# Adding expert rows to the output in DRAM with accumulating DMAs in place of a gather back

## What is computed

```python
logits = xf @ Wr + br                      # xf: the normalised 2048 rows
topv, topi = jax.lax.top_k(logits, 2)      # two of eight experts for each row
gates = jax.nn.softmax(topv, axis=-1)
...                                        # rank of each row in its expert; rows of rank >= 512 are dropped
h = jax.nn.gelu(jnp.einsum('ecd,edh->ech', xg, W1) + b1[:, None, :], approximate=False)
out = jnp.einsum('ech,ehd->ecd', h, W2) + b2[:, None, :]
weighted = out * w[..., None]
final = jnp.zeros((N + 1, C), xf.dtype).at[buf.reshape(-1)].add(weighted.reshape(-1, C))
...
x = x + final
```

## Time and profile before

| what | value |
|---|---|
| median of 3 runs | 2440.91 us (2438.87 to 2442.47) |
| span of the profiled execution | 2439.1 us |
| TensorE matmuls | 2070.7 us busy, 85% of the span |
| VectorE | 1749.3 us busy, 72% |
| ScalarE | 1053.5 us busy, 43% |
| GpSimd | 291.1 us busy, 12% |
| DMA traffic | 102.79 MB, mean 42 GB/s |
| mean granted TensorE clock | 0.912 of full speed |

### The profile page before, as it was taken

The page is one execution under the profiler, slowest core; times in us unless marked ns, Lnnn a source line. Parts: engine busy times, 40 slices in busy tenths (PEclk is TensorE's granted clock), DMA queues, the critical chain, the costliest instruction groups (busy, mean ns, idle before and its releaser), DMA issues. The chain is left out here.

```text
span 2439.1 us, 33598 instructions
## 1 busy us (share of the span) xinstructions
PE 2070.7 (85%) x12304; PEld 1268.9 (52%) x12304; DVE 1749.3 (72%) x2604; ACT 1053.5 (43%) x1646; POOL 291.1 (12%) x332
## 2 busy tenths in 40 slices
PE   4999999999999999884669778988798888669994
PEld 3666666666666666541224444444444445546662
DVE  6677777777777788769999989989899984210002
ACT  1222222222222222338666876576758842212220
POOL 1111111111111111100000000010010001310005
PEclk8999999999999999997869888978799996769997
DMA  6000000000000100011111110111101102103333
GB/s 235 2 1 18 27 26 1 18 27 26 1 18 27 31 1 1 1 56 41 52 41 36 42 52 24 37 41 35 35 24 54 52 18 78 44 20 108 108 116 112
DMA packets 57485, 102.79 MB, mean 42 GB/s; under 512 B 7828, under 2 KB 39087, under 8 KB 56832
## 3 DMA queue, kind: packets, MB, share of 16 engines
q1 hardware_dynamic: 54272, 93.67, 11.6%
q0 software_dynamic: 3072, 7.28, 1.0%
HBM read 87.10 MB, written 14.94 MB: 42 GB/s over the span
## 5 line engine op out<-in xcount | busy, mean ns | idle before, releaser
L1983 PE MATMUL pa<-arena 128*128 128x512 f32 x512 | 303.1, 722 | 93.4 <-DVE arena L1499 93.1
L1491 DVE TENSOR_TENSOR_SCAN arena<-arena 128x1024 f32<-128x1024 f32 x128 | 292.3, 2284 | 9.4 <-ACT arena L885 9.0
L1713 PE MATMUL po<-arena 128*128 128x256 f32 x960 | 224.2, 385 | 0.0
L1983 PEld LDWEIGHTS pa<-arena 128*128 128x128 f32 x512 | 102.7, 220 | 227.2 <-DVE arena L1499 125.8
L1703 PE MATMUL pa<-arena 128*128 128x512 f32 x480 | 212.4, 594 | 4.0 <-ACT arena L705 3.7
L553 POOL TENSOR_SCALAR arena<-arena 128x2 f32<-128x2 f32 (+1 forms) x92 | 27.7, 301 | 1513.9 <-DVE arena L1355 835.5
L1171 DVE TENSOR_TENSOR arena<-pa,arena 128x512 f32<-128x512 f32 x256 | 158.6, 681 | 67.3 <-PE pa L1661 67.2
L727 ACT COPY arena<-pa 128x512 f32<-128x512 f32 x128 | 65.7, 600 | 324.9 <-PE pa L1661 324.9
L869 ACT ACTIVATE arena<-arena 128x510 f32<-128x510 f32 x256 | 170.5, 717 | 59.4 <-DVE arena L1491 51.3
L1713 PEld LDWEIGHTS po<-arena 128*128 128x128 f32 x960 | 176.8, 189 | 32.8 <-issue 6.0
L1618 DVE TENSOR_TENSOR arena<-po,arena 128x512 f32<-128x512 f32 x16 | 11.1, 692 | 243.3 <-PE po L2252 217.5
(11 more groups left out here) (255 smaller groups left out, 3685.8 us busy)
## 6 DMA issues: line engine op xcount, KB each, us to landing
arena<-bc_rows SPq DMA_DIRECT2D x64, 512.0 KB, 4.4
arena<-in_L_ffn_W SPq DMA_DIRECT2D x16, 1024.0 KB, 7.3
arena<-in_L_attn_W SPq DMA_DIRECT2D x8, 1024.0 KB, 5.5
rows_to_experts<-arena SPq DMA_DIRECT2D x4, 1024.0 KB, 12.7
arena<-rows_to_experts SPq DMA_DIRECT2D x8, 512.0 KB, 8.8
rows_from_experts<-arena SPq DMA_DIRECT2D x8, 512.0 KB, 3.3
arena<-in_x SPq DMA_DIRECT2D x4, 512.0 KB, 7.6
arena<-in_rows SPq DMA_DIRECT2D x8, 256.0 KB, 3.1
```

The lines of the kernel that those rows point to most:

```text
L1491: v.tensor_tensor_scan(h.rearrange(flat), decay.rearrange(flat), h.rearrange(flat), 0.0, ALU.mult, ALU.add).then_inc(scan_done, 1)
L1713: last = mm(po[s][:, ts(i, D)], gT[:, c, ts(tile, P)], w2[:, c, :], start=c == 0, stop=c == FM - 1)
L1983: last = mm(pa[c][:, :], ident, uh[i % len(uh)][:, n, :], start=g == 0 and n == 0, stop=g == NS // NG - 1 and n == NG - 1)
```

## The change

The result is added up in DRAM. `out` gets 512 rows more behind its 2048, which serve as targets for empty slots and are cut off at the end.

- Each slot has a tag of two numbers: its token's row in `out` and its gate. A DRAM tensor `tags_to_experts` is first filled (row N + slot number within the expert, gate 0). After the last row scatter GpSimd writes tags with 32 indirect DMAs of 128 x 8 bytes, to the same slots as the rows.
- `weighed` only computes the two gates; zeroing, slot sorting and `share` are gone.
- SyncE stores x (`xst`) to `out` as soon as each pair's rows have their final value, behind the weight loads of experts 0 and 1, and one store fills the 512 extra rows. It waits for `tags_sent` behind the row loads of experts 0 and 1, then loads their slot tags; for later experts the tags follow the rows.
- VectorE gates each expert's rows in place: after an eviction (now signalled by `down3_out`, on which TensorE waits) it multiplies each of the four tiles by the gate of its slots, and signals `ye_ready` per tile. A small operation turns the tags' row numbers into integers. For expert 0 both evictions come ahead of the wait for tags.
- GpSimd adds each tile to `out` with an indirect DMA that accumulates (`compute_op=ALU.add`), four for each expert, and waits before each expert for the adds of the one before. At the end it waits for all of them.
- The gather back, the sums on VectorE, the store of expert rows and the last stores of `out` are gone.

```diff
--- before.py
+++ after.py
@@ -49,7 +49,7 @@
 HEAD_STEPS, TAIL_STEPS, CROSS_STEPS = 47, 5, 22
 CROSS_SLOTS = 38
-ROUTED_EARLY = 43
+ROUTED_EARLY = 36
 VALUE_COPIES = (0, 1, 6, 8)
@@ -325,21 +325,21 @@
     above, level = a(NT, NE, NE), a(NT, NE, NE)
     picked, before, rank = a(NT, NE), a(NT, NE), a(NT, NE)
-    lt, gate, rk, base, over, place = ([a(NT) for _ in range(2)] for _ in range(6))
-    order, part, share = ([a(NT) for _ in range(2)] for _ in range(3))
+    lt, rk, base, over = ([a(NT) for _ in range(2)] for _ in range(4))
+    tags = [a(NT, 2) for _ in range(2)]
+    gate = [one[:, :, 1] for one in tags]
     gexp = a(NT)
     into = [a(NT).bitcast(I32) for _ in range(2)]
-    outof = [a(NT).bitcast(I32) for _ in range(2)]
+    slot_tags, slot_rows = [a(TT, 2) for _ in range(2)], [a(TT).bitcast(I32) for _ in range(2)]
     weights_at = a.at
-    back = [a(NT, D) for _ in range(2)]
     assert a.at <= ARENA, a.at
     bc_rows = nc.dram_tensor("bc_rows", (BC, W), F32, kind="Internal").ap()
-    rows_back = nc.dram_tensor("rows_from_experts", (NE * CAP, D), F32, kind="Internal").ap()
+    tags_to = nc.dram_tensor("tags_to_experts", (NE * CAP, 2), F32, kind="Internal").ap()
     pa = [ctx.enter_context(nc.psum_tensor(f"pa{i}", [P, 512], F32)) for i in range(4)]
@@ -403,9 +403,9 @@
     logits_ready, sel_ready, rank_done, lt_ready, gexp_ready, places_ready = (
     scattered, tr3_done, tr3_out, up3_done, gelu3_ready = (sem(n) for n in ("scattered", "tr3_done", "tr3_out", "up3_done", "gelu3_ready"))
-    we_in, xg_in, down3_done, ye_ready, ye_kept = ([sem(f"{n}{j}") for j in range(2)] for n in ("we_in", "xg_in", "down3_done", "ye_ready", "ye_kept"))
-    back_in = [[sem(f"back_in{k}_{p}") for p in range(PAIRS)] for k in range(2)]
-    order_ready, final_ready = sem("order_ready"), sem("final_ready")
+    we_in, xg_in, down3_done, ye_ready, ye_added = ([sem(f"{n}{j}") for j in range(2)] for n in ("we_in", "xg_in", "down3_done", "ye_ready", "ye_added"))
+    down3_out, tags_in = ([sem(f"{n}{j}") for j in range(2)] for n in ("down3_out", "tags_in"))
+    tokens_in, tags_set, tags_ready, tags_sent, slot_rows_ready = sem("tokens_in"), sem("tags_set"), sem("tags_ready"), sem("tags_sent"), sem("slot_rows_ready")
     HELD[0] = sem("held")
     LAST = L * PAIRS
@@ -463,6 +463,7 @@
         for q in range(4):
+        sp.dma_start(tags_to, t["tags"]).then_inc(tags_set, 16)
         for dst, name in ((w_sv, "sim_wv"), (w_gate, "gate"), (w_pair, "pair_w"), (w_in, "ssm_in"), (w_xp, "ssm_xp"),
             sp.dma_start(dst, t[name].rearrange("(k p) n -> p k n", p=P)).then_inc(w_in_2, 16)
@@ -521,27 +522,29 @@
         def expert_rows(e, j):
-        def keep_rows(e, j):
-
-            sp.wait_ge(ye_ready[j], 2 * (e // 2) + 2)
-            sp.dma_start(rows_back[ts(e, CAP), :].rearrange("(t p) d -> p t d", p=P), ye[j]).then_inc(ye_kept[j], 16)
+        def slot_tags_in(e, j):
+            sp.dma_start(slot_tags[j], tags_to[ts(e, CAP), :].rearrange("(t p) c -> p t c", p=P)).then_inc(tags_in[j], 16)
         sp.wait_ge(xc_ready, PAIRS)
+        for one in tags:
+            sp.dma_start(one, t["tokens"]).then_inc(tokens_in, 16)
         for j in range(2):
             expert_weights(j, j)
+        sp.dma_start(out[N:N + CAP, :].rearrange("(t p) d -> p t d", p=P), xst[:, 0:TT, :]).then_inc(out_done, 16)
+        for p in range(PAIRS):
+            sp.wait_ge(xr_ready, p + 1)
+            sp.dma_start(out[p * W:(p + 1) * W, :].rearrange("(t p) d -> p t d", p=P), xst[:, TT * p:TT * p + TT, :]).then_inc(out_done, 16)
         sp.wait_ge(scattered, 16 * 2 * NT)
             expert_rows(j, j)
+        sp.wait_ge(tags_sent, 16 * 2 * NT)
+        for j in range(2):
+            slot_tags_in(j, j)
         for e in range(2, NE):
-            keep_rows(e - 2, e % 2)
+            sp.wait_ge(ye_ready[e % 2], TT * (e // 2))
             expert_weights(e, e % 2)
             expert_rows(e, e % 2)
-        for e in range(NE - 2, NE):
-            keep_rows(e, e % 2)
-        for p in range(PAIRS):
-            sp.wait_ge(final_ready, TT * p + TT)
-            sp.dma_start(out[p * W:(p + 1) * W, :].rearrange("(t p) d -> p t d", p=P), xst[:, TT * p:TT * p + TT, :]).then_inc(out_done, 16)
-        sp.wait_ge(out_done, 16 * PAIRS)
+            slot_tags_in(e, e % 2)
     def _(pool):
@@ -668,16 +671,27 @@
-        for k in range(2):
-            for j in range(2):
-                pool.wait_ge(ye_kept[j], 16 * (NE // 2 - 1 + (1 - j if k == 0 else 1)))
-            pool.wait_ge(order_ready, 2)
-            rows = CAP * (NE - 1 + k)
-            for i in range(NT):
+        pool.wait_ge(tags_set, 16)
+        pool.wait_ge(tags_ready, 2)
+        for i in range(NT):
+            for k in range(2):
                 nc.gpsimd.indirect_dma_start(
-                    out=back[k][:, i, :], out_offset=None, in_=rows_back[0:rows, :],
-                    in_offset=bass.IndirectOffsetOnAxis(ap=outof[k][:, i:i + 1], axis=0),
-                    bounds_check=rows - 1, oob_is_err=False).then_inc(back_in[k][i // TT], 16)
+                    out=tags_to, out_offset=bass.IndirectOffsetOnAxis(ap=into[k][:, i:i + 1], axis=0), in_=tags[k][:, i, :], in_offset=None,
+                    bounds_check=NE * CAP - 1, oob_is_err=False).then_inc(tags_sent, 16)
+
+        pool.wait_ge(out_done, 16 * (PAIRS + 1))
+        for e in range(NE):
+            j = e % 2
+            if e:
+                pool.wait_ge(ye_added[1 - j], 16 * TT * ((e + 1) // 2))
+            pool.wait_ge(slot_rows_ready, e + 1)
+            for i in range(TT):
+                pool.wait_ge(ye_ready[j], TT * (e // 2) + i + 1)
+                nc.gpsimd.indirect_dma_start(
+                    out=out, out_offset=bass.IndirectOffsetOnAxis(ap=slot_rows[j][:, i:i + 1], axis=0), in_=ye[j][:, i, :], in_offset=None,
+                    bounds_check=N + CAP - 1, oob_is_err=True, compute_op=ALU.add).then_inc(ye_added[j], 16)
+        for j in range(2):
+            pool.wait_ge(ye_added[j], 16 * TT * (NE // 2))
     @block.scalar
@@ -1294,22 +1308,10 @@
             dve.wait_ge(gexp_ready, ready)
+            dve.wait_ge(tokens_in, 32)
             step.after(v.tensor_scalar(gate[0][:, at], gexp[:, at], 1.0, None, ALU.add))
             step.after(v.reciprocal(gate[0][:, at], gate[0][:, at]))
-            step.after(v.tensor_tensor(gate[1][:, at], gate[0][:, at], gexp[:, at], ALU.mult))
-            for k in range(2):
-                v.scalar_tensor_tensor(gate[k][:, at], rk[k][:, at], float(CAP), gate[k][:, at], ALU.is_lt, ALU.mult)
-                last = v.scalar_tensor_tensor(place[k][:, at], rk[k][:, at], CAP - 1.0, base[k][:, at], ALU.min, ALU.add)
-            step.after(last)
-            v.tensor_tensor(outof[0][:, at], place[0][:, at], place[1][:, at], ALU.min)
-            v.tensor_tensor(outof[1][:, at], place[0][:, at], place[1][:, at], ALU.max).then_inc(order_ready, 1)
-            v.tensor_tensor(order[0][:, at], place[0][:, at], place[1][:, at], ALU.is_lt)
-            step.after(v.tensor_tensor(order[1][:, at], place[0][:, at], place[1][:, at], ALU.is_gt))
-            for k in range(2):
-
-                v.tensor_tensor(part[0][:, at], order[k][:, at], gate[0][:, at], ALU.mult)
-                step.after(v.tensor_tensor(part[1][:, at], order[1 - k][:, at], gate[1][:, at], ALU.mult))
-                step.after(v.tensor_tensor(share[k][:, at], part[0][:, at], part[1][:, at], ALU.add))
+            v.tensor_tensor(gate[1][:, at], gate[0][:, at], gexp[:, at], ALU.mult).then_inc(tags_ready, 1)
@@ -1612,24 +1614,37 @@
             for j in range(2):
                 if not first:
-                    dve.wait_ge(ye_kept[j], 16 * q)
-                for s in range(2):
+                    dve.wait_ge(ye_added[j], 16 * TT * q)
+
+                def evicted(s):
                     dve.wait_ge(down3_done[j], 2 * q + s + 1)
                     v.tensor_tensor(two(ye[j], s), po[s][:, :].rearrange("p (t d) -> p t d", t=2),
-                                    b2e[j].unsqueeze(1).broadcast_to([P, 2, D]), ALU.add).then_inc(ye_ready[j], 1)
+                                    b2e[j].unsqueeze(1).broadcast_to([P, 2, D]), ALU.add).then_inc(down3_out[j], 1)
+
+                def rows_of_slots():
+                    dve.wait_ge(tags_in[j], 16 * q + 16)
+                    v.tensor_scalar(slot_rows[j], slot_tags[j][:, :, 0], 0.0, None, ALU.add).then_inc(slot_rows_ready, 1)
+
+                def gated(s):
+                    dve.wait_ge(down3_out[j], 2 * q + s + 1)
+                    for i in (2 * s, 2 * s + 1):
+                        v.tensor_scalar(ye[j][:, i, :], ye[j][:, i, :], slot_tags[j][:, i, 1:2], None, ALU.mult).then_inc(ye_ready[j], 1)
+
+                if first and j == 0:
+                    evicted(0)
+                    evicted(1)
+                    rows_of_slots()
+                    gated(0)
+                    gated(1)
+                else:
+                    rows_of_slots()
```

(20 more changed lines are left out.)

## The result

| | before | after |
|---|---|---|
| median | 2441.69 us (4 runs, 2438.87 to 2444.74) | 2425.81 us (4 runs, 2420.99 to 2429.62) |
| span of the profiled execution | 2439.1 us | 2425.4 us |

What follows compares the result with a forecast made beforehand. TensorE was taken to bound the expert stage, with a 35 us tail behind it deciding the change. Span 2439.1 - 26.8 (tail) + 0.1 (load) = 2412.4 us, plus 1.8 to the median: 2414.2 us, range 2409 to 2422.

Steps and rivals of the forecast that it cites:

- What bounds the kernel: Expert stage: TensorE busy 28.7 of each 29.5 us; then a 35 us tail without TensorE work, which decides the change.
- The tail, removed: Behind the last matmul: storing the last rows, 16 gathers, landing, sums and output store go, 34.2 us.
- The tail, added: Behind the last eviction: gating, GpSimd's wake, last two adds, a 4.4 us landing and the end, about 7.4 us.
- The same for GpSimd: Program end: the span ends about 0.4 us after GpSimd's last wait, as it did after SyncE's.
- Adds of experts 0 to 6: Expert stage: four adds per expert, about 5.2 us of GpSimd's time in each 29.5 us, cost zero.
- Tags: Behind the last row scatter: 32 tag scatters 1.27 us apart, expert 2's weights issued about 2208, 7.4 us slack, cost zero.
- Rivals 1 and 2: Tag scatters slower than 1.50 us each delay expert 2: costing 1 to 25 us (chance 0.07), or slower than before (0.04).
- the 0 to 0.3 us for the packets beside the load: Load of expert 0's rows: tag packets running beside it add 0 to 0.3 us, taken as 0.1.
- Stores of x and gate steps: Ahead of the experts: earlier stores of x cost zero; fewer gate steps gain 0, up to 1.9 us.
- Rival 3: Adds are dear: 2 us per descriptor set, landing 8.8 us, giving 2419.6; chance 0.12 for the tail, 0.01 for pile-up.
- Rival 4: VectorE's gating and GpSimd block each other at a shared port: at worst 0.4 us on the third DMA, no chance given.
- The range: Whole time: 2409 to 2422 us, taking in rival 3 and the smaller half of rival 1.

Runs made afterwards that it cites:

- end_on_sp: The changed kernel with its last waits, for the adds to land, moved from GpSimd to SyncE: 2421.23 us, ratio 0.9920 to the kernel before.
- before_end_on_pool: The kernel before with its last wait, for the output stores, moved from SyncE to GpSimd: 2446.46 us, ratio 1.0020.
- scatter_8b: The kernel before plus eight GpSimd scatters of 128 x 8 bytes behind the row scatters, to a tensor nobody reads: 2446.85 us, one run.
- scatter_1k: The kernel before plus eight GpSimd scatters of 1 KB rows behind the row scatters, to a tensor nobody reads: 2440.91 us, one run.
- before_x_early: The kernel before with SyncE also storing x of each pair to the output early, as the changed kernel does: 2439.94 us, ratio 0.9997.
- plain_scatter: The changed kernel with plain indirect writes in place of the accumulating ones: 2442.32 us, ratio 1.0004 to the kernel before.

## Why the prediction was wrong

**What bounds the kernel**, and that the 35 us tail is where the change acts: right. TensorE's stretch from the load's landing to the last matmul kept its length: 240.0 us before (2164.08 to 2404.12), 239.9 after (2170.96 to 2410.86).

**The tail, removed** (34.2 us): right, all of it is gone.

**The tail, added.** The fourth add was to start 3.4 us behind the last matmul and started at 3.7; the gating took 0.36 us against 0.41, GpSimd's wake 0.8 against 0.86, its instruction 1.55 against 1.0. The landing was 3.8 us by the wait's end, against 4.4: the estimate from a scatter and a gather laid end to end was 0.6 too long. The step that failed is the last one, "The same for GpSimd": I took 0.4 us from SyncE's end for GpSimd's end. GpSimd closes with a drain of 6.6 us, and the old placement had hidden it behind sums and stores. The rows were there to be asked: in before this drain lasted 21.2 us and ended 1.4 us before SyncE was done. *end_on_sp* and *before_end_on_pool* show the mechanism from both sides. Mis-sized: 6.6 us.

**Adds of experts 0 to 6:** cost zero, right. They ran within each period, at 7.4 us of GpSimd's time rather than 5.2.

**Tags.** The step per tag scatter was 1.28 us, as forecast; expert 2's weights were issued at 2207.55 (forecast 2208, though all of it began 3.3 us late, so this part was about 3.7 us shorter than I put it) and its rows at 2209.57, with TensorE coming to them at 2233.89. Rivals 1 and 2, both built on a dearer step, did not occur. But the 0 to 0.3 us for the packets beside the load were wrong by a factor of ten: 3.6 us. I had counted bytes, and *scatter_8b* against *scatter_1k* shows that bytes are not the measure: the packets of the load itself grew longer beside the small ones. The Trainium skill, *DMA: Bandwidth & Descriptors*, specifications, says that a transfer under 512 B is done as a read and a write. I weighed that rule only for GpSimd's own step, where the trace did not show it; the loads beside 8-byte and 1 KB pieces (7.06 and 4.05 us) agree with it in that small pieces cost more than their bytes, and its place was the shared load. What happens inside an engine no run shows.

**Stores of x and gate steps:** cost and gain nothing, right. For the stores *before_x_early* shows it; for both, the cross attention took the same 81.6 to 81.7 us before and after wherever the clock was alike.

**The rivals.** Rival 3 (dear adds) had the right place and the wrong thing: its time, 2419.6, was closer than the forecast, but landing and instruction were near my values, and plain writes were no faster. Rival 4 left no trace in the result.

**The range** was too narrow at the top by 4 us: it lacked the drain, and also the spread between executions, for the start of the experts' part alone wanders by 9 us. With 0.4 replaced by 7.0 us at the end (2418.4 to 2425.4), 0.1 by 3.6 at the load, 4.4 by 3.8 at the landing and the fourth add 0.3 later, the sum is 2414.2 + 6.6 + 3.5 - 0.6 + 0.3 = 2424.0 us; measured were 2425.8 and 2423.8.

## What to carry to other kernels

When a change moves an engine to the end of a program, ask the trace how that engine closes: a GpSimd queue that has issued DMAs drained for 5 to 8 us here, free while others work and bare once it is last. A final wait was better placed on an idle queue. Put a stream of tiny writes where no transfer on the critical path shares the DMA engines with it; holding 32 of them back until that transfer had landed gave back 3.5 us in the profile. And where two medians differ by a few us, compare the stretch that was edited and not the whole: 2.1 us at the end could be read in the profile and not in the time.

## What the runs showed of the hardware beyond that

- An accumulating indirect DMA of 128 rows of 1 KB to DRAM took 1.55 us of GpSimd's time against 0.97 for a plain one, and was seen to land 3.8 to 4.0 us after its start when nothing else ran, against 2.5 for a plain one at the same place.
- ScalarE and VectorE can be released late while GpSimd issues indirect DMAs. In *plain_scatter* it was 17.0 us at ScalarE; in the kernel before it is the eviction at 2401.14 in rows 3, which came 4 us late beside the gathers (its matmuls were through at 2397.19), hidden by the second half. Of the five profiles with that set of gathers four show it at the same place (before, the end on GpSimd, 8 bytes, 1 KB) and one does not (the early stores of x). What delays the release was not found out.
